# Storing the finished gated units of a quantised gated feed-forward as magnitudes, and forming every signed gated unit anew in the down pass

## The reference, cut to what matters

```python
def act_qdq(x):
    qmax = 2.0 ** (ACT_BITS - 1) - 1.0
    scale = jnp.maximum(jnp.max(jnp.abs(x)) / qmax, 1e-12)
    return jnp.clip(jnp.round(x / scale), -qmax - 1.0, qmax) * scale
...
x = act_qdq(x)
up = act_qdq(x @ lpbq_dequant(w_up).T)
gate = act_qdq(x @ lpbq_dequant(w_gate).T)
sig = fixed_qdq_u16(jax.nn.sigmoid(gate))
gate = act_qdq(gate * sig)
o = act_qdq(gate * up)
return o @ lpbq_dequant(w_down).T
```

## Time and profile before

| what | before |
|---|---|
| median of 3 runs | 2325.39 us (2324.28 to 2326.08) |
| the profiled execution, its own time | 2322.58 us |
| its span, first to last instruction | 2320.7 us |
| PE, DVE, ACT, POOL busy | 88%, 72%, 60%, 25% |
| gate pass on PE, from 620.8 us | 500 us |
| up pass on PE, 1120.8 to 1618.1 us | 497 us |
| PE idle between up and down pass | 193.1 us |
| down pass on PE, from 1811.6 us | 498 us |

### The profile page before, as it was taken

How to read it: one execution, slowest core, us unless ns; L and a number is a source line. 1 busy time by engine, 2 the same in 40 slices (tenths; PEclk the granted TensorE clock), 3 DMA queues, 4 the chain that set the end, 5 groups by cost and what they waited for, 6 DMA issues and landing times.

```text
span 2320.7 us, 25770 instructions
## 1 busy us (share of the span) xinstructions
PE 2031.3 (88%) x9780; PEld 975.5 (42%) x9780; DVE 1678.2 (72%) x1385; ACT 1401.9 (60%) x1599; POOL 578.9 (25%) x600
## 2 busy tenths in 40 slices
PE   5899999998699999999999999998000799999998
PEld 2455555554344444444444444444000344444443
DVE  8799999999444443532699997999899644488641
ACT  4588888886322322322698995666899643467530
POOL 2587777776100000000112111222110000000000
PEclk9999999999799999999999999999555899999999
DMA  7689999997348647633899994787998755545641
GB/s 294 261 312 364 361 366 364 355 371 300 136 167 267 258 164 230 223 144 141 299 393 382 376 363 176 295 322 288 414 417 328 284 227 216 205 195 218 236 154 73
DMA packets 131163, 634.63 MB, mean 273 GB/s; under 512 B 12256, under 2 KB 12768, under 8 KB 91104
## 3 DMA queue, kind: packets, MB, share of 16 engines
q1 hardware_dynamic: 85888, 316.81, 37.3%
q0 software_dynamic: 45152, 316.16, 34.8%
HBM read 430.69 MB, written 202.24 MB: 273 GB/s over the span
## 4 chain that ended last, share of the span: by engine, by line
PE 64%; DVE 3%; issue 3%; ACT 2%; POOL 0%; DVEq 0%; ACTq 0%; POOLq 0%
PE fd_pp L1778 43%; PE fd_pp L1792 21%; ACT ff_ring L1721 1%; DVE ff_sig L1576 1%; DVE ff_h_parts L1560 1%; DVE ff_sq L1498 1%; ACT ff_sig L1708 0%; DVE ff_sq L1567 0%; DVE kept_gate L1569 0%; DVE ff_gin L1511 0%; DVE ff_hq L1550 0%; ACT ff_ring L1747 0%; ACT ff_sig L1737 0%; ACT ff_hq L1633 0%; DVE kept_o_peak L1576 0%
## 5 line engine op out<-in xcount | busy, mean ns | idle before, releaser
L1792 PE MATMUL fd_pp<-ff_down,kept_gate 128*128 128x512 f16 x1536 | 457.9, 380 | 193.1 <-DVE ff_up L1617 193.1
L1778 PE MATMUL fd_pp<-ff_h_parts,kept_gate 128*128 128x512 f16 x2304 | 500.4, 381 | 14.7 <-DVE ff_h_parts L1416 14.7
L1778 PE MATMUL fd_pp<-ff_h_parts,ff_up 128*128 128x512 f16 x2304 | 497.4, 379 | 0.0
L1640 ACT ACTIVATE ff_raw<-fd_pp 128x1024 f32<-128x1024 f32 x192 | 194.3, 1017 | 397.4 <-PE fd_pp L1778 397.4
L1778 PEld LDWEIGHTS fd_pp<-ff_h_parts,kept_gate 128*128 128x128 f16 x2304 | 226.1, 98 | 288.8 <-DVE ff_h_parts L1416 15.0
L1778 PEld LDWEIGHTS fd_pp<-ff_h_parts,ff_up 128*128 128x128 f16 x2304 | 225.4, 98 | 271.8
L1421 DVE TENSOR_REDUCE kept_gate_peak<-ff_raw 128x1 f32<-128x2048 f32 x48 | 109.7, 2285 | 293.5 <-ACT ff_raw L1640 293.5
L1792 PEld LDWEIGHTS fd_pp<-ff_down,kept_gate 128*128 128x128 f16 x1536 | 150.4, 98 | 375.2 <-issue 194.7
L1792 PE MATMUL fd_pp<-ff_down,ff_up 128*128 128x512 f16 x768 | 291.6, 380 | 0.0
L1747 ACT ACTIVATE ff_ring<-ff_hq,kept_g 128x2048 int16<-128x2048 f32 x48 | 96.0, 1999 | 189.5 <-DVE ff_hq L1550 188.2
L787 PE MATMUL at_psO<-kept_wo,at_ahi 128*128 128x512 f16 x512 | 154.9, 384 | 15.9 <-ACT at_alo L278 10.1
(11 more groups left out here) (239 smaller groups left out, 3311.8 us busy)
## 6 DMA issues: line engine op xcount, KB each, us to landing
ff_raw<-up_scratch SPq DMA_DIRECT2D x66, 1024.0 KB, 8.5
gate_scratch<-ff_raw POOLq DMA_DIRECT2D x48, 1024.0 KB, 9.1
ff_gin<-gate_scratch SPq DMA_DIRECT2D x48, 1024.0 KB, 8.4
up_scratch<-ff_raw POOLq DMA_DIRECT2D x48, 1024.0 KB, 6.8
ff_gin<-gate_integers SPq DMA_DIRECT2D x73, 512.0 KB, 6.3
gate_integers<-ff_ring POOLq DMA_DIRECT2D x43, 512.0 KB, 8.7
ff_up<-up_scratch SPq DMA_DIRECT2D x21, 1024.0 KB, 9.1
kept_xs<-in_x SPq DMA_DIRECT2D x32, 512.0 KB, 12.3
```

The lines of the kernel that those rows point to most:

```text
L1640: nc.scalar.activation(raw[:, n % UNITS, h * 2 * BLK:(h + 1) * 2 * BLK], pp[(2 * n + h) % 4][:, :, :].rearrange("p a t -> p (a t)"), ACT.C ...
L1778: mm = nc.tensor.matmul(pp[k % 4][:, h, :], wt[w][:, c, f:f + P], a[:, b % 2, :, c, :], start=(q == 0), stop=(q == len(todo) - 1))
L1792: mm = nc.tensor.matmul(pp[k % 8 // 2][:, k % 2, :], a[b % 2][:, f, t * P:(t + 1) * P], wt[w][:, f, :], start=(q == 0 and i == 0), stop=(q ...
```

## The change

Five things change together.

1. In the gate pass DVE also takes the greatest signed gate of each unit (a second reduction over `raw`).
2. In the first part of the up pass ACT makes all the gate integers, one unit ahead. The magnitude of the gate is no longer made: the fused multiply and maximum runs on the integers with the factor -1, which finds the greatest magnitude among negative gates; the greatest positive one is worked out once from the greatest gate (three instructions on one element per partition). The kept units' integers are stored here too.
3. In the last part 40 units (READY) are finished in place of 36, of which 10 stay in SBUF in place of 8. ACT's sigmoid is followed at once by an Abs in place, so that DVE forms magnitudes. 21 of them are stored, to a tensor of their own (`gate_m`), and `gate_q` keeps the gate integers.
4. The product pass has 8 late steps in place of 12: ACT makes sigmoid and Abs together three steps ahead, and DVE finishes the unit two steps ahead. No other unit needs a magnitude there. 29 gated units are loaded. NEAR and AHEAD keep their values.
5. In the down pass all 48 units are loaded as gate integers, and each gets a sigmoid on ACT, its 16-bit integers and the scaled signed unit on DVE (`last_gated`). The first two are done before the scale of `o` is taken up.

```diff
-READY = 36
+READY = 40
-KEPT = 8
+KEPT = 10
...
-    WQ, NEAR = 4, 7
+    WQ, NEAR = 2, 7
...
+                    if n < NU:
+                        nc.vector.tensor_reduce(keep["gate_top"][:, n:n + 1], raw[:, n % UNITS, :], AX.X, ALU.max)
...
-                    nc.vector.tensor_tensor_reduce(out=sig[:, u % 2, :], in0=ab[:, u % 2, :], in1=sq[:, :], scale=1.0,
+                    nc.vector.tensor_tensor_reduce(out=sig[:, u % 2, :], in0=integers(u), in1=sq[:, :], scale=-1.0,
...
+                def second(v, a, t):
+                    sigmoid_integer(NU + v, a)
+                    dve.wait_ge(m["mag"], v + 1)
+                    nc.vector.scalar_tensor_tensor(out=t, in0=sq[:, :], scalar=g[:, 7:8], in1=t,
                                                    op0=ALU.mult, op1=ALU.mult).then_inc(m["g2"], 1)
...
+                def last_gated(k):
+                    dve.wait_ge(m["fsig"], k + 1)
+                    need(dve, m["fgq"], k)
+                    nc.vector.tensor_scalar(sq[:, :], sig[:, k % 2, :], 65536.0, 65535.0, ALU.mult, ALU.min).then_inc(m["fsq"], 1)
+                    dve.wait_ge(m["fsq"], k + 1)
+                    need(dve, m["fo"], k - 1)
+                    nc.vector.scalar_tensor_tensor(out=fo_gq[:, k % 2, :], in0=sq[:, :], scalar=g[:, 7:8], in1=wide[:, k % FG, :],
+                                                   op0=ALU.mult, op1=ALU.mult).then_inc(m["fgq"], 1)
...
                 for i in range(-2, NU):
                     k = i + 2
                     if k < NU and made[k] == "late":
+                        second(READY + nth(k), 0, gated(k))
...
                 opk_v(dve)
+                last_gated(0)
                 last_product(0)
+                last_gated(1)
...
                 for n in range(-3, NU + UNITS):
                     k = n + 5
+                    if k < NU:
+                        last_gated(k)
...
+                def first(u):
+                    gate_integers(u + 1)
                     need(act, m["gpeak"], u - 1)
-                    nc.scalar.activation(ab[:, u % 2, :], gin[:, u % GR, :], ACT.Abs, scale=g[:, 5:6]).then_inc(m["ab"], 1)
...
                     if k < NU and made[k] == "late":
                         x = nth(k)
-                        have_gated(act, k)
+                        act.wait_ge(g_in[g_slot[k][0]], 16 * uses(g_slot, loaded, k))
                         act.wait_ge(m["sq"], NU + READY + x)
                         nc.scalar.activation(sig[:, 0, :], gated(k), ACT.Sigmoid, scale=g[:, 4:5]).then_inc(m["sig"], 1)
+                        nc.scalar.activation(gated(k), gated(k), ACT.Abs).then_inc(m["mag"], 1)
...
-                    k = i + 1
-                    if 0 <= k < NU and made[k] == "act":
-                        have_gated(act, k)
-                        nc.scalar.activation(gated(k), gated(k), ACT.Abs).then_inc(m["ga_act"], 1)
-                    if 0 <= k < NU and made[k] == "late":
-                        act.wait_ge(m["gp"], nth(k) + 1)
-                        nc.scalar.activation(gated(k), late_gp, ACT.Abs, scale=g[:, 7:8]).then_inc(m["ga_late"], 1)
...
                 last_up(0)
+                last_sigmoid(0)
                 last_up(1)
+                last_sigmoid(1)
+                last_sigmoid(2)
                 act.wait_ge(m["o_scales"], 1)
```

More of the change, by code:

```diff
@@ L969, in feed @@
             home.append(where)
-            made.append("done" if v in DONE else "dve" if made.count("act") > 2 * made.count("dve") else "act")
+            made.append("ready")
     def nth(i):
@@ L1083, in second_units @@
             return [v for v in range(READY) if SECOND + v // 2 == n]
-        def magnitude_at(n):
-            return [v for j, v in enumerate(DONE) if n == SECOND + max(3 + j if v < KEPT else 0, v // 2 + 2)]
         def kept(j):
-            return spare[:, j, :] if j < 6 else more[:, j - 6, :]
+            return spare[:, j, :] if j < 6 else more[:, j - 6, :] if j < 8 else ab[:, j - 8, :]
         def integers(u):
@@ L1106, in stored_first, with late_at @@
             return len(range(r, AWAY, QR))
+        def late_at(x):
+            return [i for i in range(NU) if made[i] == "late"][x]
         def have_gq(eng, u):
[L1110 to L1113, removed]
+            eng.wait_ge(m["gq"], u + 1)
         def gq_free(eng, u):
@@ L1131, in sq_free @@
                 need(eng, m["gpeak"], k)
-            elif k <= NU + READY:
+            else:
                 eng.wait_ge(m["g2"], k - NU)
[L1134 to L1138, removed]
         def gated(i):
@@ L1143, in gated @@
             if kind == "wq":
-                return hq[:, j, :] if j < 2 else ab[:, j - 2, :]
+                return hq[:, j, :]
             return again(j - AWAY if j >= AWAY else j + KEPT)
@@ L1150, in have_gated @@
                 eng.wait_ge(g_in[g_slot[i][0]], 16 * uses(g_slot, loaded, i))
-            else:
+            if made[i] == "late":
+                eng.wait_ge(m["g2"], READY + nth(i) + 1)
+            elif home[i] != "load":
                 u = order[i]
                 eng.wait_ge(m["g2"], (u - AWAY if u >= AWAY else u + KEPT) + 1)
[L1154 to L1165, removed]
         def u_slot(i):
@@ L1175, in fg_free @@
         def fg_free(eng, n):
[L1177 to L1180, removed]
+            eng.wait_ge(m["fgq"], n + 1)
         with nc.Block() as block:
@@ L1357, in load_gated @@
                         pool.wait_ge(again_out[u % AR], 16 * (u // AR + 1))
-                    pool.dma_start(gated(i), gate_q[u]).then_inc(g_in[kind, j], 16)
+                    pool.dma_start(gated(i), (gate_q if late(u) else gate_m)[u]).then_inc(g_in[kind, j], 16)
                 soon = [i for i in loaded[:WQ] if late(order[i])]
@@ L1686, in _ @@
                 act.wait_ge(m["hq"], NB)
+                gate_integers(0)
                 for n in range(NU):
+                    if n == 1:
+                        act.wait_ge(m["top"], 1)
+                        nc.scalar.activation(top_s[:, :], top_i[:, :], ACT.Sigmoid, scale=g[:, 4:5]).then_inc(m["top_s"], 1)
                     for u in first_units(n)[:1]:
@@ L1697, in _ @@
                     evict(NU + n, 1)
-                    for v in magnitude_at(n):
-                        magnitude(v)
                 AHEAD = 3
```

155 lines of the change are left out of this document (57 added, 98 removed).

## The result

| what | before | after |
|---|---|---|
| median of 4 runs, side by side | 2324.84 us | 2369.46 us |
| lowest to highest | 2323.17 to 2326.08 | 2368.36 to 2373.13 |
| ratio, 95% interval | | 1.0195 (1.0178 to 1.0213) |
| profiled execution, span | 2322.58, 2320.7 | 2373.13, 2371.4 |

The account below looks back on a forecast made before the run. PE was taken as full in the gate, up and down passes, leaving the product pass and down-pass start to change: 0.9 + 10.4 = +11.3 us on 2325.39, about 2336.7 us, range 2320 to 2348.

Parts of the forecast that it names:

- The gate pass, nothing: Gate pass: 48 more DVE reductions of 2.285 us cost nothing while PE is the pace.
- The up pass, first part, nothing: Early up pass: DVE loses two of three gate conversions, ACT 48 Abs for 32 conversions; lighter, so no time change.
- The up pass, last part, nothing: Late up pass: ACT's 9.4 us and DVE's 93% fit PE's 10.4 us unit; no change, 1 us a unit spare.
- The rival on the up pass: Late up pass: ACT-to-DVE hand-overs cost 1.3 us more, 20 units lose 0.3 us each; +6 on top, 2343; chance 0.02.
- The product pass, +0.9: Between up and down pass: a late-load loop sets the pace, last product ends at 1802.9 against 1802.0 before.
- the cycle: Product pass: six steps from one late load to the next, load time plus 14.2 us, taken as 21.9 us.
- L: Product pass: time a late load takes to land, taken as 7.7 us; 27 such loads ranged 3.9 to 10.3.
- The start, +10.4: Last product to PE's down-pass start: a chain of 20.0 us against 9.6 before.
- The rest of the down pass, nothing: Down pass after its start: DVE's 8.6 us a unit fits in PE's 10.4, so no change.
- Sign and range: Whole kernel: slower (chance 0.71), +11.3 us to about 2336.7, range 2320 to 2348 us.
- The rule weighed: Product pass: if 358 GB/s bound HBM to SBUF, 8.3 MB takes 23.2 us, pass ends at 1812; given little weight.

Follow-up runs that it names:

- all four edits: Changed kernel with h loads two units earlier on SP, product-pass loads ten ahead (NEAR 10), down-pass start reordered, x loads on POOL: 2303.12 us, 0.9910.

## Why the prediction was wrong

- **The gate pass, nothing:** right. PE is full in all 500 us.
- **The up pass, first part, nothing:** right, 316.6 of 316.6 us.
- **The up pass, last part, nothing: this step failed, by 32 us.** It weighed ACT (9.4 of 10.4 us a unit) and DVE, and those held: in the run with the h loads first PE was full beside them. It wrote "SP two loads more" and gave that no cost. It did not ask what stands behind a waiting load on SP, though the split of every block hangs on a load there: the runs show the h load held 38 us behind reloads that wait for stores, three waits of PE (18.2 us), and 8 us of lower clock. The rival on the up pass was about the wrong engine. By stages it is 26.5 us in the pass and 5.4 behind it.
- **The product pass, +0.9:** right. With the late splits out of the way it took 183.3 us from PE's last matmul, against 183.6 before. ACT waited 2.5 to 4.5 us where 3 to 5 were named, the cycle was 21.6 to 22.1 us where 21.9 was worked out, and L, where 7.7 was taken, was 7.7 on the mean of the seven loads. DVE was 78% busy (147.4 of 188 us), under the 85% named. Three slips in its sums are too small to matter: the listed terms of the cycle add to L + 14.1, those of the start to 19.8, so the sum would read +10.4 in place of +11.3; and its 3.9 gated loads in six steps are those of the old 31 loads, with 29 it is 3.6.
- **The start, +10.4:** right, 20.1 us where 20.0 was worked out.
- **The rest of the down pass, nothing: this step failed too, by 6 us.** DVE's 8.6 of 10.4 us was enough, as the run with x on POOL shows. What was missed is again on SP. In the kernel before ACT waited 37.2 us for the integers of its 12 sigmoids behind the same loads of x, and PE lost nothing; with 48 sigmoids it waited 119.9 us, and DVE's sums left PSUM too late for PE.
- **Sign and range:** slower was right. With the stall of the up pass taken out the kernel runs at 2336.94 us, and the forecast was 2336.7; but in that run's profile the start is 10.6 us longer and the down pass 4.8, 14.2 us of span in all, while the medians differ by 11.0. That the medians agree to the last us is luck.
- **The rule weighed:** the 358 GB/s of the Trainium skill's "DMA: Bandwidth & Descriptors" does not bind here. With all four edits the pass drew 408 and 418 GB/s for 164 us. The Trainium skill's "HBM Reference", section "Specifications (TRN2)", has about 425 GB/s for a core that streams alone, and these runs agree with that.

## What to carry to other kernels

When a change alters how many buffers are kept, work out for every load that waits for a store whether the store now comes later than the load's place in its queue, and list what is queued behind it: here an order that cost nothing in the old kernel cost 32.5 us in the new one, and moving two lines took it back. Read from the trace how far ahead of its use each load on such a queue is issued (20.5 us for h), and hold any slip against that. A change that loses can still be the better design: with its waits gone, this one is 16.6 us faster than the old kernel at the best order tried for it.

## What the runs showed of the hardware

After a wait of 4.59 us PE's granted clock was 0.50 in the first 4 us and 0.90 in the next 4, so a stall costs more than its length. The DMA engines held 418 GB/s at a share of 1.02 through a stretch of 83 us. And with the loads of x on POOL's queue the end behind PE's last matmul was 4.5 to 4.7 us shorter in both kernels, though the last stores were issued at the same pace. The difference lies in one instruction at the end of POOL's program, DRAIN, which the views by busy time leave out. The rows of its line give durations in ns and the start; here the kernel before, and then the same with x on POOL:

```profile
L1182 POOLq DRAIN  x1: 5124/5124/5124, 2314.1 to 2314.1; - x1
```
```profile
L1182 POOLq DRAIN  x1: 632/632/632, 2316.5 to 2316.5; - x1
```

It took 5.1 to 5.3 us in all seven profiles with x on SP and 0.63 us in all five with x on POOL. Why it is longer there stays open.
